# Copying the scan carries of two units at once in a Mamba layer with a quantised feed-forward block

## The reference

```
xz = in_proj(x);  x, z = split(xz)
x = silu(causal_conv(x));  dt, B, C = x_proj(x);  dt = softplus(dt_proj(dt))
for every token t, channel d, state n:
    h[d,n] = exp(dt[t,d] * A[d,n]) * h[d,n] + dt[t,d] * B[t,n] * x[t,d]
    y[t,d] = sum_n h[d,n] * C[t,n]
out = out_proj((y + x*D) * silu(z));  x1 = layernorm(x + out)
result = layernorm(x1 + W2q @ relu(W1q @ x1 + b1) + b2)
```

## Time and profile before

| | |
|---|---|
| median of 3 runs | 4861.68 us (4856.44 to 4863.53) |
| the profiled execution | 4863.47 us, of which the span of its instructions is 4861.4 us |
| mean granted clock of TensorE | 0.968 of full speed |
| PE busy | 4458.8 us (92% of the span) |
| DVE busy | 3926.1 us (81%) |
| ACT busy | 3613.7 us (74%) |
| POOL busy | 3188.2 us (66%) |
| scans L933 | 2048, mean 1268 ns |
| dbu L627 | 1024, mean 2412 ns |
| carries L601 | 1022, mean 278 ns |

### The profile page before, as it was taken

The page is one execution under the profiler, slowest core; times in us unless marked ns, Lnnn a source line. Parts: engine busy times, 40 slices in busy tenths (PEclk is TensorE's granted clock), DMA queues, the critical chain, the costliest instruction groups (busy, mean ns, idle before and its releaser), DMA issues.

```text
span 4861.4 us, 85854 instructions
## 1 busy us (share of the span) xinstructions
PE 4458.8 (92%) x23618; PEld 3170.0 (65%) x23618; DVE 3926.1 (81%) x4654; ACT 3613.7 (74%) x6854; POOL 3188.2 (66%) x2471
## 2 busy tenths in 40 slices
PE   6989898989898989989898989898988899999998
PEld 2656565656566666656565656565656588888887
DVE  4989898989898989889898989898989754444444
ACT  4888988889898989898989898989897522222222
POOL 3898978797979888888888888888888300000000
PEclk7999999999999999999999999999999999999999
DMA  2333333333333333323333333333333200000000
GB/s 92 97 104 101 105 103 103 101 103 105 106 100 108 102 106 99 113 92 117 101 109 99 111 94 115 102 105 111 97 131 128 66 27 35 35 35 35 35 35 35
DMA packets 233380, 436.78 MB, mean 90 GB/s; under 512 B 23968, under 2 KB 24096, under 8 KB 232416
## 3 DMA queue, kind: packets, MB, share of 16 engines
q1 hardware_dynamic: 232928, 431.55, 28.0%
HBM read 397.38 MB, written 34.08 MB: 89 GB/s over the span
## 4 chain that ended last, share of the span: by engine, by line
PE 33%; POOL 27%; issue 18%; ACT 13%; DVE 6%; POOLq 1%; DMA 1%; ACTq 0%; DVEq 0%; SPq 0%
POOL dbu L627 22%; PE ht L1365 8%; PE y L1378 5%; PE gemm L1378 5%; ACT ch L688 4%; PE ht L1229 4%; PE gemm L1177 4%; ACT decay L674 3%; PE y L1234 3%; DVE h L933 3%; PE gemm L1213 2%; POOL x L561 2%; POOL carry L601 1%; PE gemm L1204 1%; POOL dtx L574 1%
## 5 line engine op out<-in xcount | busy, mean ns | idle before, releaser
L933 DVE TENSOR_TENSOR_SCAN h<-decay,carry,dbu 128x512 f32<-128x512 f32 x2048 | 2519.7, 1268 | 292.2 <-ACT decay L674 188.8
L627 POOL TENSOR_TENSOR dbu<-dtx,bb 128x1024 f32<-128x1024 f32 x1024 | 2470.3, 2412 | 8.7 <-issue 4.1
L674 ACT ACTIVATE decay<-dt,aneg 128x512 f32<-128x512 f32 x2048 | 1438.9, 705 | 221.6 <-DVE h L933 209.0
L1229 PE MATMUL ht<-ident,h 128*128 128x128 f32 x8192 | 1256.5, 282 | 346.8 <-ACT ch L688 237.7
L1229 PEld LDWEIGHTS ht<-ident,h 128*128 128x128 f32 x8192 | 970.9, 144 | 865.4 <-ACT ch L688 391.5
L688 ACT ACTIVATE ch<-ht,ct 128x256 f32<-128x256 f32 x3456 | 1461.8, 485 | 80.5 <-PE ht L1229 79.4
L1177 PE MATMUL gemm<-xt,win 128*128 128x512 f32 x2048 | 1014.6, 605 | 12.1 <-DMA win<-w_in 7.2
L1234 PEld LDWEIGHTS y<-ident,ch 128*128 128x128 f32 x6912 | 818.4, 144 | 228.0 <-issue 223.2
L1234 PE MATMUL y<-ident,ch 128*128 128x128 f32 x6912 | 923.9, 278 | 0.4 <-ACT ch L688 0.4
L853 ACT ACTIVATE hr<-ht,b1c 128x512 f32<-128x512 f32 x256 | 176.3, 689 | 707.3 <-PE ht L1365 707.3
L601 POOL TENSOR_TENSOR carry<-h,ones_pair 128x2 f32<-128x2 f32 x1022 | 283.7, 278 | 514.2 <-DVE h L933 501.8
(11 more groups left out here) (91 smaller groups left out, 3923.6 us busy)
## 6 DMA issues: line engine op xcount, KB each, us to landing
bb<-b_rows SPq DMA_DIRECT2D x1024, 256.0 KB, 3.5
win<-w_in SPq DMA_DIRECT2D x256, 256.0 KB, 2.6
xt<-x_cm SPq DMA_DIRECT2D x16, 1024.0 KB, 9.3
xres<-x_tm SPq DMA_DIRECT2D x16, 1024.0 KB, 7.6
x<-xres SPq DMA_DIRECT2D x16, 1024.0 KB, 5.2
xr<-x SPq DMA_DIRECT2D x16, 1024.0 KB, 5.4
out<-xr SPq DMA_DIRECT2D x16, 1024.0 KB, 4.3
raw<-w SPq DMA_DIRECT2D x8, 1024.0 KB, 7.6
```

The lines of the kernel that those rows point to most:

```text
L627: nc.gpsimd.tensor_tensor(dbu[:, u % 2, :, :], dtx[:, pair(q), :], bb[:, u % BB_RING:u % BB_RING + 1, :].to_broadcast([P, 2, TC]), ALU.mul ...
L674: nc.scalar.activation(DA[j][:, :], dt[:, c.par, i, :], ACT.Exp, scale=aneg[:, i, n:n + 1])\
L933: nc.vector.tensor_tensor_scan(h[:, H_SLOT[u], j, :], DA[j][:, :], dbu[:, u % 2, j, :], carry[:, c.par, n, i:i + 1], ALU.mult, ALU.add).th ...
L1229: ins = nc.tensor.transpose(HT[k][:, tb % 2, j * P:(j + 1) * P], h[:, H_SLOT[u], j, tb * P:(tb + 1) * P], ident[:, :])
```

## The change

`save_state` becomes `save_states`: at odd units from 3 on, one GpSimd product copies the last columns of units u - 3 and u - 2 (four elements per partition in place of two). At unit 1 it does so for the last two units of the chunk before. At even units dbu stands alone. `carried` thus counts 32 in a chunk in place of 64. `h` has four buffers, unit u uses buffer u % 4. `dtx` holds two pairs of blocks in place of four; the wait in `make_dtx` is for dbu of the pair two before. `xhi` of the feed-forward part lies over `z` and waits for the first four gates of the last chunk.

```diff
-H_SLOT = [u % 3 for u in range(UNITS - 4)] + [1, 0, 2, 1]
+H_RING = 4
+H_SLOT = [u % H_RING for u in range(UNITS)]
+CARRIES = UNITS // 2
...
-        ones = sb("ones_pair", [P, 2])
+        ones = sb("ones_pair", [P, 2, 2])
...
-        dtx = sb("dtx", [P, NB, TC])
+        dtx = sb("dtx", [P, 2, 2, TC])
...
-        h = sb("h", [P, 3, 2, TC])
+        h = sb("h", [P, H_RING, 2, TC])
...
-        xhi = over("xhi", [P, KM, TC], "dtx", HALF, F32R)
+        xhi = over("xhi", [P, KM, TC], "z", 0, F32R)
...
             def make_dtx(f, i):
-                wait(pool, dbu_ready, f, UNITS, (i // 2 - NP + 1) * NS)
+                wait(pool, dbu_ready, f, UNITS, (i // 2 - 1) * NS)
...
-                nc.gpsimd.tensor_tensor(dtx[:, i, :], dt[:, f.par, i, :], x[:, f.par, i, :], ALU.mult)\
+                nc.gpsimd.tensor_tensor(dtx[:, i // 2 % 2, i % 2, :], dt[:, f.par, i, :], x[:, f.par, i, :], ALU.mult)\
...
-            def save_state(c, u):
+            def save_states(c, u):
                 q, n = u // NS, u % NS
-                wait(pool, scanned, c, SCANS, 2 * u + 2)
-                nc.gpsimd.tensor_tensor(carry[:, c.par, n, pair(q)], h[:, H_SLOT[u], :, TC - 1], ones[:, :], ALU.mult)\
-                    .then_inc(carried, 1)
+                wait(pool, scanned, c, SCANS, 2 * u + 4)
+                nc.gpsimd.tensor_tensor(carry[:, c.par, n:n + 2, pair(q)], h[:, H_SLOT[u]:H_SLOT[u] + 2, :, TC - 1],
+                                        ones[:, :, :], ALU.mult).then_inc(carried, 1)
...
-                    if u >= 2:
-                        save_state(c, u - 2)
-                    elif not is_first:
-                        save_state(p, UNITS - 2 + u)
+                    if u % 2 and u >= 3:
+                        save_states(c, u - 3)
+                    elif u == 1 and not is_first:
+                        save_states(p, UNITS - 2)
...
-                    nc.gpsimd.tensor_tensor(dbu[:, u % 2, :, :], dtx[:, pair(q), :],
+                    nc.gpsimd.tensor_tensor(dbu[:, u % 2, :, :], dtx[:, q % 2, :, :],
...
+            wait(act, gated, last, NB, KM)
...
-                    wait(dve, carried, c.near(back), UNITS, user + 1)
+                    wait(dve, carried, c.near(back), CARRIES, user // 2 + 1)
```

More of the change, by code:

```diff
@@ L82, in h_user_before @@
     return -1, max(v for v in range(UNITS) if H_SLOT[v] == H_SLOT[u])
-COUNTS = sorted({1, 4, 8, 16, 64, 128, 256, 2 * len(BY_ACT), len(BY_ACT), TB * len(BY_DVE), NB * (KC - 1)})
+COUNTS = sorted({1, 4, 8, 16, CARRIES, 64, 128, 256, 2 * len(BY_ACT), len(BY_ACT), TB * len(BY_DVE), NB * (KC - 1)})
 KINDS = {"x": NB, "z": NB, "xd": 1, "ct": 1, "dt": NB, "o": TB}
@@ L547, in _ @@
         def _(pool):
-            nc.gpsimd.memset(ones[:, :], 1.0).then_inc(consts_set, 1)
+            nc.gpsimd.memset(ones[:, :, :], 1.0).then_inc(consts_set, 1)
             nc.gpsimd.memset(epsln[:, :], EPS_LN).then_inc(consts_set, 1)
@@ L826, in _ @@
             wait(act, dbu_ready, last, UNITS, UNITS)
-            wait(act, carried, last, UNITS, UNITS - 2)
+            wait(act, carried, last, CARRIES, CARRIES - 1)
+            wait(act, gated, last, NB, KM)
             act.wait_ge(bias_in, 32)
@@ L1121, in _ @@
                 if n == 1:
-                    wait(dve, carried, last, UNITS, UNITS - 2)
+                    wait(dve, carried, last, CARRIES, CARRIES - 1)
                     split_lo(0)
```

## The result

The changed kernel takes 4885.04 us in the median of 5 runs (4881.92 to 4886.40), the kernel before 4863.32 us (4856.44 to 4864.48, 5 runs). The profiled execution took 4884.31 us with a span of 4882.3 us, 20.9 us more than before.

What follows compares the result with a forecast made beforehand. No engine has room; GpSimd mostly follows VectorE, and what moves the logarithms' start moves the chunk's rest. 4863.5 + 34.7 - 6.8 - 2.4 = 4889.0 us, less 1.8 for the median: 4887.2 us, range 4852 to 4897.

Steps and rivals of the forecast that it cites:

- The new collision: Unit 10: without its carry, dbu runs between VectorE's lift and rounding; VectorE 2.17 us late, 34.7 us over 16 chunks.
- Rival (B): VectorE's rounding at unit 10 keeps the interface, so no new wait and the gains stay: 4852.5 us; chance 0.24.
- Step (e): Units 14 to 36: VectorE stands only 0.7 us in 86 us, so no lost time is made up there.
- (d): Unit 10: ScalarE's two logarithms and table loads start when its second scan ends, so delay there moves the chunk's rest.
- (C): dbu goes first, but TensorE's 2.9 us in hand and unseen slack cover VectorE's 2.17 us: 4861.7 us; chance 0.10.
- The gains: Removed carries give back 0.15 us each: 6.8 us at 15 chunk turns, 2.4 us after the logarithms, 9.2 us together.
- what I gave the carries before units 62 and 0: Chunk turn: carries gone before dbu of units 62, 0 and 4 save 0.15 us each, 0.45 us at 15 turns.
- the start of the sum: Starting time of the forecast: profiled execution of 4863.5 us, with the median of the runs 1.8 us below it.
- VectorE's busy time: Whole run: VectorE's busy time grows by some 35 us though it does nothing more.
- the exchange at unit 56: Unit 56: dbu now goes ahead of the sum of dt and no longer ahead of the shift, which comes out even.
- Step (f): After unit 36, ScalarE leads to unit 60.
- (D): Paired copy does not shorten GpSimd's queue, its waits hiding all, while the collision stays: 4896 us; chance 0.04.

Runs made afterwards that it cites:

- The kernel before with a single swap: Kernel before, with the carry of unit 8 issued behind dbu of unit 10 instead of in front: 4901.01 us, ratio 1.0074.
- the small product: Changed kernel plus one unread two-element GpSimd product directly in front of dbu of unit 10: 4848.11 us, ratio 0.9969 to the kernel before.
- the kernel with the rounding moved: Changed kernel with the fourth pair's rounding at position 29, behind the second scan of unit 9, instead of 27: 4867.02 us, ratio 1.0010 to the kernel before.
- The wait at unit 56: dbu of unit 56 also waits for the first sum of dt: 4842.79 us added to the kernel before, 4824.59 us added to the kernel with the small product.
- the even-unit kernel: Changed kernel with the paired copies at even units, so odd units have no carry: 4869.41 us, ratio 1.0014 to the kernel before.
- The buffers: Changed kernel's buffers (four scan buffers, two dt*x pairs, xhi over z) but a carry for each unit: 4860.85 us, ratio 0.9998 to the kernel before.
- unit 17 without a copy: Kernel with the small product, with the paired copy of unit 17 issued behind dbu instead of in front: 4890.78 us, ratio 1.0063 to the kernel before.

## Why the prediction was right

**The new collision.** It decided the sign, and its working held line by line: the rounding of unit 9 at 2.85 us (forecast about 2.9), dbu at 3.34 us (3.3), dbu's end 2.22 us after the lift's (2.21), the rounding's end 0.56 us after that (0.56), 2.0 to 2.3 us lost between the scans of units 8 and 9 in each of 16 chunks (forecast 2.17; the lift before the rounding is itself 0.1 to 0.2 us longer or shorter than it was). The kernel before with a single swap shows it alone (+38 us) and the small product takes it away (-37 us), where 34.7 were forecast: cause and size are shown from both sides. The decay behind the logarithms comes 2.0 us later in the chunks that are not behind a turn, where I had some 1.7. Rival (B), VectorE keeping the interface, is refuted for this place.

**That nothing is made up behind it.** Step (e) held. In the kernel with the swap, counted from unit 8 of the same chunk, the scans are 2.17 us late at unit 9 and 2.1 to 3.1 us late at units 36 and 57, in 15 chunks; the last chunk alone makes some up (1.5 and 1.2 us). At unit 11 it is 1.4 us, since the scan there used to wait 0.65 us for dbu, and at unit 12 2.17 us again, since the decay behind the logarithms is late by all of it. That is what (d) said. Three chunks get 1.1 us back between units 58 and 60, and three others lose 0.8 us more there. The 2.9 us that TensorE had in hand covered nothing, so (C) falls.

**The gains.** The sum had 9.2 us; the kernel with the small product has 4863.0 - 4848.1 = 14.9 us. The 0.15 us is right: between scans 12 and 14 the time falls by 0.12 to 0.16 us in 14 of 16 chunks of the changed kernel, and from unit 3 to unit 8 by 0.2 to 0.3 in the same number. Two sizes were off. Units 0 to 4 of the chunks behind a turn of the loop got shorter by up to 1.8 us, with a large spread (0.1 to 1.8 over seven turns, 1.3 in the middle), while those of the other chunks got 0.13 us shorter. And what I gave the carries before units 62 and 0 in the other chunks is lost again at the turn of the loop. Why the units behind a turn gain more than their carries is not settled: no run isolates the turn. Much of it may be spread: the kernel with the rounding moved has the same instructions in units 0 to 4 and takes 18.4 to 18.8 us for them in the six chunks that begin where the loop has gone back, the changed kernel 17.1 to 18.6, the kernel before 18.5 to 19.9.

**The nearness of the time.** The total fitted better than its terms. The collision cost 36.9 us between the changed kernel and the one with the small product (34.7 in the sum), the gains 14.9 us (9.2 in the sum), so the change was worth 21.7 us and not 25.5. Another 1.6 us came from the start of the sum: three runs of the kernel before had a median of 4861.68 us, five have 4863.32. That no more than 2 us remain is luck. The chunks that are not behind a turn of the loop came to 234.3 to 235.9 us (forecast 235), those behind one to 235.5 to 238.2 us (forecast 238).

**VectorE's busy time.** I said some 35 us more; it was 21.6. The roundings grew by 27.8 us (34.7 at unit 9, less 7 at units 4 and 52, where they stand behind a GpSimd that is done sooner) and the sums by 29.0 us, but the shift shrank by 30.5 us and the scans by 5.3. Sums and shift are the exchange at unit 56, which comes out even, as forecast; what the 35 left out is the 7 us and the scans. VectorE and then GpSimd in the changed kernel:

```profile
2174.43 3.37 DVE L922 SCALAR_TENSOR_TENSOR dt<-soft,dt 128x1024 f32<-128x1024 f32 x1 [0.90 <-POOL soft L568]
2177.72 0.15 DVE L987 SCALAR_TENSOR_TENSOR shift<-mv,rstd 128x4 f32<-128x4 f32 x1
...
2174.36 2.35 POOL L629 TENSOR_TENSOR dbu<-dtx,bb 128x1024 f32<-128x1024 f32 x1
```

Sum and shift end 3.44 us after the sum's start; in the earlier trace rows it was 3.46.

**Step (f), that ScalarE leads up to unit 60, failed.** It did not enter the sum, but it hid the best thing in the profile. A VectorE operation of four elements took 2.32 us, and I took what happens there as covered. The wait at unit 56 gained 16 us in the kernel before and 23.5 us in the one with the small product, and the even-unit kernel lost 21 us in the same stretch. ScalarE stands idle there before a decay until the scan behind the shift has run; only after that does it lead. In the kernel before:

```profile
2163.23 0.69 ACT L674 ACTIVATE decay<-dt,aneg 128x512 f32<-128x512 f32 x1 [1.34 <-DVE h L933]
```

This idle time is there in 14 chunks (1.33 or 1.34 us each) and in none of the kernel with the wait.

**The rest.** The buffers at 0: 0.9998. The copy of four elements costs about what one of two does: 201 ns in the median against 191 (the means, 261 and 278, have the waits in them). I had said 0.2 us for every copy and 512 of them; they are 511, and 55 still last over 0.3 us. (D) asked for no gain at all, and there were 15 us.

## What to carry to other kernels

Where VectorE runs two operations in a row of the kinds that GpSimd and VectorE shut each other out of here (lift, sum, shift, rounding; not the scans), look at what GpSimd has waiting when the first ends: if it is a long operation, the second can stand for all of it. A short operation in front, a wait that holds the long one back, or another place for the second operation removes that, and an operation on GpSimd that looks like waste may be what keeps the two apart. Rows in which a small operation lasts as long as a large one of the other engine are the places to look, before any engine's share of busy time.

## What the runs showed of the hardware

GpSimd waiting behind one VectorE operation went ahead of the next in nearly all cases: 16 of 16 between lift and rounding (changed kernel), 15 of 15 between rounding and lift (even units), 14 of 14 between sum and shift (kernel before), 15 of 15 between the sums (unit 17 without a copy). But between the sums in the even-unit kernel it was 2 of 15, with the same two instructions, and in 14 of the 15 chunks dbu was issued 0.16 us into the first sum, as there. So the order of issue does not settle it alone; a margin cannot be relied on where it has not been measured.

A dbu that waited behind one VectorE operation ended 2.20 to 2.24 us after it, where alone it takes 2.36, and a rounding that waited ended 0.54 to 0.56 us after GpSimd's operation, where alone it takes 0.67. This held in the traces of all twelve kernels.
